# A loop of attention over two-batch groups, reordered into rounds: all half-array matmuls of a round in one run, with four score banks and two query banks

## The reference, cut to what matters

```python
q_big = einsum('bshk,hkq->bshq', (layernorm(x) @ Wq.T).reshape(B, S, H, K), w_kc_q)
q_big = _apply_rope(q_big, sin_q, cos_q)                       # width 192 per head
q_r, k_r = einsum('bshq,hqr->bhsr', q_big, W_qr), einsum('bld,hdr->bhlr', kv_r, W_kr)
attn = softmax(einsum('bhsr,bhlr->bhsl', q_r, k_r))
ctx_c = einsum('bhsl,bld->bhsd', attn, kv_r)
x = x + einsum('bhsd,hkd->bhsk', ctx_c, w_kc_kv)...reshape(B, S, H * K) @ Wo.T
```

## Time and profile before

| | us |
|---|---|
| median of 3 runs | 413.5 |
| lowest, highest | 413.28, 413.62 |
| span of the profiled execution | 411.3 |
| its TensorE busy time | 386.1 (94%) |
| its VectorE busy time | 306.3 (74%) |
| its ScalarE busy time | 216.8 (53%) |
| its GpSimd busy time | 180.6 (44%) |
| the loop's first scores to the last tile of the attention's output | 32.4 to 275.9 |

### The profile page before, as it was taken

One profiled execution on the slowest core, in us unless ns is written; L12 is line 12 of the kernel. 1 busy time (PEld: TensorE's weight loads), 2 busy tenths in 40 slices (PEclk: granted clock), 3 DMA queues, 4 the chain that ended last, 5 costly groups with the idle time before them and its releaser, 6 DMA issues.

```text
span 411.3 us, 6289 instructions
## 1 busy us (share of the span) xinstructions
PE 386.1 (94%) x2121; PEld 257.6 (63%) x2121; DVE 306.3 (74%) x676; ACT 216.8 (53%) x579; POOL 180.6 (44%) x170
## 2 busy tenths in 40 slices
PE   8799899999999999999999999988879988999996
PEld 8675556656666666566655677764245445678886
DVE  5796777877767668776668766646989998898673
ACT  1523655555465657556553876327879532574140
POOL 2554456555646554664656422386530042053200
PEclk9999999999999999999999999999977999999999
DMA  7638001020020030000210000300000000000001
GB/s 254 202 125 328 1 22 81 1 104 2 2 102 2 0 104 1 2 0 0 81 63 0 2 0 0 114 0 2 0 1 0 2 0 0 2 1 2 26 27 52
DMA packets 9087, 17.54 MB, mean 43 GB/s; under 512 B 2144, under 2 KB 6944, under 8 KB 8160
## 3 DMA queue, kind: packets, MB, share of 16 engines
q1 hardware_dynamic: 9056, 17.14, 12.4%
HBM read 16.09 MB, written 1.05 MB: 42 GB/s over the span
## 4 chain that ended last, share of the span: by engine, by line
PE 61%; DVE 22%; ACT 9%; issue 4%; DMA 2%; POOL 1%; SPq 0%; DVEq 0%; ACTq 0%
PE bank L1340 7%; PE bank L1464 7%; PE bank L1458 6%; PE bank L1433 6%; PE bank L1342 6%; PE bank L1341 6%; PE bank L1446 5%; DVE rot_up L891 4%; PE bank L1418 3%; ACT prob L629 3%; PE bank L1363 3%; DVE relu L1050 2%; ACT probT L620 2%; PE bank L1412 2%; DMA blobs<-in_blob 2%
## 5 line engine op out<-in xcount | busy, mean ns | idle before, releaser
L462 POOL TENSOR_TENSOR prob<-prob,rinv 128x512 f32<-128x512 f32 x64 | 67.0, 1048 | 106.5 <-DVE rinv L956 106.5
L629 ACT ACTIVATE prob<-bank,negmax 128x256 f32<-128x256 f32 x128 | 60.1, 480 | 39.8 <-DVE negmax L951 39.8
L951 DVE TENSOR_REDUCE negmax<-bank 128x2 f32<-128x512 f32 x64 | 41.2, 686 | 25.1 <-PE bank L1433 24.6
L620 ACT COPY probT<-bank 128x512 f32<-128x512 f32 x64 | 37.8, 591 | 19.2 <-PE bank L1446 19.0
L457 POOL TENSOR_TENSOR rot_low<-rot_low,rot_up 128x512 f32<-128x512 f32 x32 | 40.8, 1276 | 10.9 <-DVE rot_up L891 10.9
L891 DVE TENSOR_TENSOR rot_up<-bank,cb 64x512 f32<-64x512 f32 x64 | 44.1, 689 | 0.9
L1340 PE MATMUL bank<-xnT,w 128*128 128x512 f32 x96 | 42.0, 437 | 2.2 <-DVE xnT L867 1.7
L1446 PEld LDWEIGHTS bank<-ca,prob 128*128 128x128 f32 x256 | 30.5, 141 | 18.8 <-issue 16.1
L889 DVE TENSOR_TENSOR rot_low<-bank,cb 128x512 f32<-128x512 f32 x32 | 22.0, 688 | 25.2 <-PE bank L1342 25.1
L1446 PE MATMUL bank<-ca,prob 128*128 128x128 f32 x256 | 38.9, 275 | 1.8 <-ACT probT L620 1.1
L442 POOL TENSOR_TENSOR c_y<-c_ve,minus_half 128x4 f32<-128x4 f32 (+1 forms) x9 | 9.8, 1087 | 64.9 <-DVE c_ve L848 52.1
(11 more groups left out here) (213 smaller groups left out, 788.3 us busy)
## 6 DMA issues: line engine op xcount, KB each, us to landing
blobs<-in_blob SPq DMA_DIRECT2D x7, 1024.0 KB, 4.9
xs<-in_x SPq DMA_DIRECT2D x2, 512.0 KB, 4.1
xn<-in_w_fc_t SPq DMA_DIRECT2D x1, 1024.0 KB, 4.8
ctxT<-in_w_proj_t SPq DMA_DIRECT2D x1, 1024.0 KB, 5.5
out<-qk SPq DMA_DIRECT2D x8, 128.0 KB, 1.8
cb<-in_const_b SPq DMA_DIRECT2D x1, 768.0 KB, 8.5
blobs<-in_w_gate SPq DMA_DIRECT2D x1, 704.0 KB, 4.3
blobs<-in_w_up SPq DMA_DIRECT2D x1, 704.0 KB, 5.7
```

The costliest lines, as they stand in the source:

```text
L462: pool.tensor_tensor(p[:], p[:], rinv[:, n % PROBS, :].unsqueeze(2).to_broadcast([P, 2, S]), ALU.mult).then_inc(normed, 1)
L620: act.copy(probT[n % 2][:].rearrange("p a s -> p (a s)"), pT[:]).then_inc(probsT_copied, 1)
L629: ins = act.activation(prob[n % PROBS][:, st, :], pS[n % 2][:, st * S:(st + 1) * S], ACT.Exp, bias=negmax[:, n % 2, st:st + 1], accum_out= ...
L951: dve.tensor_reduce(negmax[:, n % 2, :], pS[n % 2][:].rearrange("p (a s) -> p a s", a=2), AX, ALU.max, negate=True).then_inc(max_ready, 1)
```

## The change

The slots are gone. The loop is written out as rounds, one for each group `g` (0 to 15). On TensorE a round begins with `small_tiles`: `latent_u(g+1, 0)`, fold 3 where there is one, the contexts of both batches of group g-1, the scores of both batches of group g. Then come whole-array matmuls only: `latent_q`, `latent_u(g+1, 1)`, `latent_q`, the first unit's transposes, a fold, the second unit's, `latent_q`, the third's, a fold, the fourth's. The line numbers that follow for the changed kernel are its own: 1536 own product, 1577 contexts, 1552 scores, 1436 to 1438 `latent_q`, 1523 `latent_u(.., 1)`, 1568 transposes, 1470, 1477 and 1481 folds 0 and 1, 2, and 3.

Banks: scores in four (1, 3, 5, 6), one for each unit; `latent_q` alternately in 0 and 7, so that it waits for the rope before the last one; contexts in the transposes' bank 4, both batches in one, copied at once; folds 0 to 2 in `pu` (bank 2), fold 3 in bank 0. Folds 0 and 1 of a pair stand in the even rounds, fold 2 in the odd ones, fold 3 in the even round after. With it come new waits: `prep(p, 1)` and the next round's `latent_u(.., 0)` wait for VectorE's `w1_low` to be through with `pu` (`w1_parts`), and round 13's for the weights' scale (`wscale_ready`). The projection and the weights' casting follow in rounds 14 and 15.

```diff
+UNITS = 4
+PROBS = UNITS
+SCORE_BANK = (1, 3, 5, 6)
...
+def folds_at(g):
+    p = g // 2 + 2
+    if p >= PAIRS:
+        return (None, None)
+    return ((p, 0), (p, 1)) if g % 2 == 0 else ((p, 2), None)
+def late_fold_at(g):
+    p = g // 2 + 1
+    return p if g % 2 == 0 and 2 <= p < PAIRS else None
...
+        pq, pu, pT = [bank[0], bank[7]], bank[2], bank[4]
+        pS, pV, last_pV = [bank[i] for i in SCORE_BANK], bank[4], [bank[5], bank[6]]
         def fold_bank(f, i):
-            return bank[i] if f == 0 and i < 3 else pW
+            if f < 2:
+                return bank[i] if f == 0 and i < 3 else bank[7]
+            return pu if i < 3 else pq[0]
...
+            return bank[Q_BANK[m]] if m < QSTEPS else pq[m % 2]
...
+            for g in range(GROUPS):
+                n = g + 2
+                norm_probs(UNITS * g)
+                norm_probs(UNITS * g + 1)
+                if n < GROUPS:
+                    join(n, 0)
+                norm_probs(UNITS * g + 2)
+                norm_probs(UNITS * g + 3)
+                if n < GROUPS:
+                    join(n, 1)
+                    join(n, 2)
...
+            for g in range(QUIET):
+                n = UNITS * g
+                if late_fold_at(g) is not None:
+                    fold_copy(late_fold_at(g), 3)
+                if g:
+                    context_copy(g - 1)
+                exponentials(n)
+                exponentials(n + 1)
+                exponentials(n + 2)
+                u_copy(g + 1)
+                turned_probs(n)
+                exponentials(n + 3)
+                first, second = folds_at(g)
+                if first is not None:
+                    fold_copy(*first)
+                turned_probs(n + 1)
+                turned_probs(n + 2)
+                if second is not None:
+                    fold_copy(*second)
+                turned_probs(n + 3)
+                if g in WD_ROUNDS:
+                    wd_round(WD_ROUNDS.index(g))
...
+            n = UNITS * QUIET
+            context_copy(QUIET - 1)
+            exponentials(n)
+            exponentials(n + 1)
+            w8_cast(0)
+            exponentials(n + 2)
+            u_copy(QUIET + 1)
+            turned_probs(n)
+            exponentials(n + 3)
+            w8_cast(1)
+            turned_probs(n + 1)
+            w8_cast(2)
+            turned_probs(n + 2)
+            w8_cast(3)
+            turned_probs(n + 3)
+            for j in range(4, W8_PIECES):
+                w8_cast(j)
...
+            for g in range(QUIET):
+                n, m = UNITS * g, RT * (g + 2)
+                first, second = folds_at(g)
+                largest_score(n)
+                largest_score(n + 1)
+                largest_score(n + 2)
+                inverse_sum(n)
+                rope_straight(m)
+                inverse_sum(n + 1)
+                rope_crossed(m)
+                largest_score(n + 3)
+                inverse_sum(n + 2)
+                rope_straight(m + 1)
+                inverse_sum(n + 3)
+                rope_crossed(m + 1)
+                if first is not None and first[1] < 2:
+                    w1_low(*first)
+                if g == SCALE_ROUND:
                     dve.wait_ge(wmax_turned, 1)
-                    in_order(dve.tensor_reduce(wcol[:], pW[:, 0:P], AX, ALU.max))
+                    in_order(dve.tensor_reduce(wcol[:], pu[:, 0:P], AX, ALU.max))
                     dve.tensor_scalar(wdiag[:], ident[:, 0:2], wcol[:], None, ALU.mult).then_inc(wdiag_ready, 1)
-                if s == SCALE_AT + 4:
+                rope(m + 2)
+                if second is not None:
+                    w1_low(*second)
+                if g in (1, 2):
+                    weight_largest(g - 1)
+                if g in WD_ROUNDS:
...
+                elif i == 0:
+                    if f == 1:
+                        pe.wait_ge(wkvo_ready, 1)
+                    else:
+                        pe.wait_ge(u_copied, 2 * f - 2)
+                elif i == 1:
+                    pe.wait_ge(w1_parts, 2 * f + 1)
+                elif i == 2:
+                    if f == 1:
+                        pe.wait_ge(w1_parts, 2 * f + 2)
+                    else:
+                        pe.wait_ge(u_copied, 2 * f - 1)
+                elif f == 1:
                     pe.wait_ge(wqk_ready, f + 1)
-                elif i == 3:
-                    pe.wait_ge(turned_copied, 4)
+                else:
+                    pe.wait_ge(rot_ready, RT * (2 * f - 2) + 5)
...
+                if m > QSTEPS + 1:
+                    pe.wait_ge(rot_ready, m - 1)
+                    if m % RT == 0 and late_fold_at(m // RT - 2) is not None:
+                        pe.wait_ge(wkvo_ready, late_fold_at(m // RT - 2) + 1)
...
+                if 2 <= n < GROUPS - 2:
+                    if n % 2:
+                        pe.wait_ge(wqk_ready, n // 2 + 2)
+                    else:
+                        pe.wait_ge(w1_parts, n + 4)
+                elif n == GROUPS - 2:
+                    pe.wait_ge(wscale_ready, 1)
...
+                    at = a * S + st * P
                     for h in range(2):
                         lo, hi = h * DC, (h + 1) * DC
-                        ins = pe.matmul(pS[h][:, st * S:(st + 1) * S], uT[b // 2][lo:hi, at:at + P],
+                        ins = pe.matmul(pS[2 * a + h][:, st * S:(st + 1) * S], uT[g % 2][lo:hi, at:at + P],
                                         ktmp[lo:hi, b * S:(b + 1) * S], start=True, stop=True)
                         if st == 1:
...
+            def small_tiles(g):
+                if g + 1 < GROUPS:
+                    latent_u(g + 1, 0)
+                if late_fold_at(g) is not None:
+                    prep(late_fold_at(g), 3)
+                if g:
+                    contexts(g - 1)
+                if g == 0:
+                    pe.wait_ge(kv_ready, 2)
+                scores(g, 0)
+                scores(g, 1)
...
+            for g in range(QUIET):
+                n, m = UNITS * g, RT * (g + 2)
+                first, second = folds_at(g)
+                small_tiles(g)
+                latent_q(m)
+                latent_u(g + 1, 1)
+                latent_q(m + 1)
+                turn_probs(n)
+                if first is not None:
+                    prep(*first)
+                if g == SCALE_ROUND:
                     pe.wait_ge(wmax_ready, 2)
-                    pe.wait_ge(wkvo_ready, PAIRS)
-                    pe.transpose(pW[:, 0:P], pad, ident).then_inc(wmax_turned, 1)
-                if s == SCALE_AT + 3:
+                    pe.wait_ge(u_copied, g + 2)
+                    pe.transpose(pu[:, 0:P], pad, ident).then_inc(wmax_turned, 1)
+                turn_probs(n + 1)
+                latent_q(m + 2)
+                turn_probs(n + 2)
+                if second is not None:
+                    prep(*second)
+                if g == SCALE_ROUND:
                     pe.wait_ge(wdiag_ready, 1)
-                    pe.matmul(pW[:, P:P + 2], ones, wdiag[:], start=True, stop=True).then_inc(wmax_here, 1)
-                if s >= LAST_PAIR:
-                    for n in range(AHEAD * (s - LAST_PAIR), AHEAD * (s - LAST_PAIR + 1)):
-                        if n < 6 * (PAIRS - 1):
-                            project_ahead(n)
-                if s > LAST - AHEAD:
-                    for n in range(AHEAD * (s - LAST + AHEAD - 1), AHEAD * (s - LAST + AHEAD)):
-                        if n < 2 * (PAIRS - 1):
-                            project_ahead(6 * (PAIRS - 1) + n)
-                if last_pair_at(s) is not None:
-                    project_last(last_pair_at(s))
-                if batch_at(s) is not None:
-                    if batch_at(s) == 0:
-                        pe.wait_ge(kva_ready, 1)
-                    context(batch_at(s))
-                if unit_at(s - TURN_AFTER) is not None:
-                    turn_probs(unit_at(s - TURN_AFTER))
+                    pe.matmul(pu[:, P:P + 2], ones, wdiag[:], start=True, stop=True).then_inc(wmax_here, 1)
+                turn_probs(n + 3)
...
+            n = UNITS * QUIET
+            small_tiles(QUIET)
+            latent_u(QUIET + 1, 1)
+            ahead(0, 4)
+            turn_probs(n)
+            ahead(4, 8)
+            turn_probs(n + 1)
+            ahead(8, 12)
+            turn_probs(n + 2)
+            ahead(12, 16)
+            turn_probs(n + 3)
+            ahead(16, 34)
...
+            n = UNITS * (QUIET + 1)
+            small_tiles(QUIET + 1)
+            ahead(34, 42)
+            turn_probs(n)
+            ahead(42, 44)
+            turn_probs(n + 1)
+            project_last(0)
+            turn_probs(n + 2)
+            ahead(44, 46)
+            turn_probs(n + 3)
+            project_last(1)
+            last_contexts()
+            ahead(46, 50)
+            project_last(2)
+            ahead(50, NT * (PAIRS - 1))```

```

(56 more changed lines are left out.)

269 lines of the change are left out of this document (107 added, 162 removed).

## The result

The kernel after takes 423.98 us (median of 4 runs, 421.26 to 424.9), the kernel before, measured beside it, 413.39 (4 runs, 413.0 to 413.62): a ratio of 1.0218, with a 95% interval from 1.0164 to 1.0272. It is slower, and the forecast of 424 stands within 0.1. The profiled execution is the quickest of the four: 421.26, with a span of 419.5. Against the span of 411.3 before that is +8.2, where the sum said +11; the agreement of the medians is better than the sum was, and the end of "why" says where the rest lies. Three of the four runs are 2.1 to 3.6 slower than this one, so in what follows gains are read from spans and from the starts of rounds, not from medians alone.

What follows compares the result with a forecast made beforehand. TensorE, nearly always busy, bounds the kernel before; after, chains through the other engines set the rounds. +14.0 to round 14's scores and -3.0 in the tail give +11 on 413.5: 424 forecast, range 412 to 430.

Steps and rivals of the forecast that it cites:

- the sum: Whole profiled execution: +14.0 us up to round 14's scores, -3.0 in the tail, so +11 on the span of 411.3.
- here `w1_low` stands on the path: End of even rounds: both folds' low parts, 0.61 each, hold up the next own product; in bank 7 they cost nobody anything.
- One sign that the prediction named: Wait before the own product: put down to VectorE's line 908 in even rounds, GpSimd's line 448 in odd ones.
- The changes of form: TensorE switching between half-array and whole-array work: eight per group become three, 5.15 becomes 4.74, saving some 0.9 us a group.
- Even rounds: Loop rounds with folds 0 and 1: crossed half ends at 12.90, then low parts, third rope, low parts: 16.3 us.
- Odd rounds: Loop rounds whose next own product waits for GpSimd's join after the crossed half ends at 12.46: 13.9 us.
- TensorE alone: Odd round: TensorE's own work would be through at 12.5, so it stands still for 1.4 us.
- it does what it is built for: Rival: TensorE stays the bound in the loop, pairs of 26.2, whole kernel 394 us; chance 11%.
- Round 12: Next own product waits for the weights' scale: 12.90, small steps some 0.5, rope 2.09, last scale steps 1.1: 16.6 us.
- Round 13: Near the loop's end, taken like round 1: 13.9 us.
- given back: Tail from round 14's scores to the output's last tile: 3.5 less TensorE work, 0.5 of stalls, so 3 us back.
- the clock falls: Rival: stops in the rounds drop TensorE's clock, ten us at half clock per pair, 30 us more, 454; chance 4%.

Runs made afterwards that it cites:

- first experiment: Kernel after the change with folds 1 and 2 exchanged, so fold 1's low parts stand in the odd round: 415.05 us, ratio 1.0052 to the kernel before.
- second experiment: Kernel after the change with the weights' scale split over rounds 12 and 13: 419.62 us, ratio 1.0143 to the kernel before.
- third experiment: Both moves together: kernel after the change with folds 1 and 2 exchanged and the weights' scale split over rounds 12 and 13: 409.94 us, ratio 0.991.
- fifth experiment: Kernel after the change without the low parts of the loop's folds (pairs 2 to 7), output not the reference's: 410.23 us, ratio 0.9932 to the kernel before.
- fourth experiment: Kernel after the change with VectorE's fourth reciprocal behind the crossed half in even rounds: 418.76 us, ratio 1.0137 to the kernel before.
- sixth experiment: Kernel after the change with folds back in bank 7 and one bank for latent_q instead of two: 473.44 us, ratio 1.1431 to the kernel before.

## Why the prediction was right, and where it was not

**The shape.** The order of the waits, the alternation, the run of own product, fold 3 and contexts, and VectorE's 4 us of idleness came as forecast. The first experiment moves the second fold's low parts away, with no work taken out; the waits of 8.4 for them are gone and each even round is 1.3 shorter: the step "here `w1_low` stands on the path" is shown, not only argued. One sign that the prediction named is half right: the wait ahead of the own product is put down to line 908 at the end of even rounds, as forecast, but at the end of odd ones no matmul's wait is put down to line 448; only the load of the own product's weights waits for it, 0.2 in each of seven rounds.

**The changes of form.** Own product, two batches' contexts and scores were to take 4.74; from 134.62 to the next `latent_q` at 139.28 they take 4.66. Against the 5.15 of before the saving is there in full, and by the first transposes the round is 0.2 ahead of the forecast (8.41 and 8.84 after the start, forecast 8.61 and 9.05). Here the trace agrees with the Trainium skill's "TensorEngine Tiling (Array Packing)", Key Properties; and, as the prediction held against it, the rule tells nothing of who waits next.

**Even rounds: 16.06, forecast 16.3.** The 0.2 are those of TensorE's first part; from the transposes on, the chain to the crossed half's end took 3.76 (127.40 to 131.16), forecast 3.85.

**Odd rounds: 13.58, forecast 13.9.** 0.2 again by the early transposes, and 0.1 by a shorter chain. But the term beside it was wrong: TensorE alone was to be through at 12.5, so that it would stand for 1.4. It stands for 0.77 only, and ahead of line 1568. The sum had the last two transposes 0.36 apart. They are 1.37 apart (146.25 to 147.62), since both go through one bank: the second waits until ScalarE has copied the first. That is 1.0; 0.16 more is the fold (0.93, not 0.77) and the rest the starts. With ScalarE's copy in it, TensorE's part alone needs 13.58, not 12.5. The rival "it does what it is built for" was overrated by the same step: its pair of 26.2 takes the odd round at 12.5 and the even one at 13.7. With both moves made the pair is 28.38: 1.1 more in the odd round by the above, and 1.1 more in the even one, 0.6 of it the wait for the first low parts and most of the rest the two folds of 0.93. Whether the join or the copy sets the odd round stays open. They end within 0.05, the matmul rows name the copy and the weight load names the join, and no experiment moved one without the other.

**Round 12: 17.48, forecast 16.6.** The mis-sized term is the small steps of the scale, which were taken from the 0.17 of a reciprocal: 0.5 for two. The profile after (VectorE and GpSimd):

```profile
220.11 0.29 DVE L1055 TENSOR_REDUCE wcol<-bank 128x1 f32<-128x128 f32 x1
220.16 1.26 POOL L448 TENSOR_TENSOR rot_low<-rot_low,rot_up 128x512 f32<-128x512 f32 x1 [0.37 <-DVE rot_up L947]
...
220.44 1.01 DVE L1056 TENSOR_SCALAR wdiag<-ca,wcol 128x2 f32<-128x2 f32 x1
221.36 0.68 DVE L941 TENSOR_TENSOR rot_z<-bank,cb 128x512 f32<-128x512 f32 x1
...
223.52 1.26 POOL L446 TENSOR_TENSOR rot_z<-rot_z 128x512 f32<-128x512 f32 x1 [2.10 <-DVE rot_z L947]
...
223.87 0.94 DVE L1069 TENSOR_SCALAR wsi<-wsi 128x2 f32<-128x2 f32 x1
```

From line 1055's start to the rope's start it is 1.25 instead of 0.5, and line 1069 takes 0.94 where line 983 took 0.72: 1.0 together, with 0.14 of hand-over; the crossed half ends 0.3 earlier than forecast. The operations themselves are not slow. In the kernel before, the one of line 1056 takes 0.23:

```profile
216.94 0.23 DVE L977 TENSOR_SCALAR wdiag<-ca,wcol 128x2 f32<-128x2 f32 x1
```

No operation of GpSimd runs beside it there. After the change one does, and both steps end 0.02 to 0.03 after GpSimd's operation: 221.44 after 221.42, 224.81 after 224.78. The 0.72 before is the same (222.95, GpSimd's ends at 222.93). So 0.5 for the small steps was right for a VectorE that has GpSimd idle beside it. What the sum lacked is that after the change both stand next to a join.

**Round 13: 15.27, forecast 13.9.** In the second and third experiments, where no fall of the clock stands there, the round takes 13.7. The fall costs 1.7, and the last section shows it.

**Sums.** Round 14 starts at 240.22, forecast 241.9; its scores (243.02 in the last chain) come 12.3 later than before, forecast 14.0. The output's last tile (line 1099) is at 284.30, so that scores to last tile take 41.3, before 45.2: 3.9 given back, forecast 3.0. That makes +8.4, the span +8.2.

**The rest of the median.** By the medians the kernel is 10.6 slower, by the spans 8.2. The three runs that were not profiled have spans of 421.6, 422.8 and 423.1 with a mean granted clock of 0.984, 0.975 and 0.976, against 419.5 and 0.988 in the profiled one: the time goes with the clock. The rival "the clock falls" had 4% and a price of 30 us. It was right in kind and far off in size: in the profiled execution one fall in the loop costs 1.7. Where the clock fell in the other three runs no profile tells. The lowest and highest run lie 3.6 apart in the kernel after, 4.0 and 4.2 in the first and fifth experiments, which keep the scale's 2.6 of waiting, and 1.0 and 1.25 in the third and second, which don't. But the kernel before has no such stop either, and its 17 runs beside the experiments lie 3.9 apart; and the part behind the attention, with falls of its own, takes 135.0 to 136.3 in profiled executions of kernels that are alike there. So it stays open whether the clock's loss in those three runs hangs on this stop.

The forecast of the median was thus met by luck, by two errors of opposite sign: the span was forecast 2.8 too long (4.5, had the fall in round 13 not come), and the distance from the profiled span to the median 2.3 too short (2.2 kept, 4.5 measured).

## What to carry to other kernels

When like work is gathered into runs, ask of each bank it shares who reads it last, and where in that engine's queue the reading stands: 0.62 of low parts cost nothing in one round and 1.3 in the other, where a rope of 2.1 came onto the path with them. Two uses of one bank in a row cost the copy between them (1.37 instead of 0.36), even if neither engine is full. When a small step of VectorE is put on the path, look at what GpSimd does at that time: the same step took 0.23 alone and 1.01 beside a join. A saving on the engine that bounds the kernel (here 0.9 a group) is worth only what is left after the chain through the others, so follow that chain to the end of the round before counting it, and move single steps rather than speed them up.

## What the runs showed of the hardware

The granted clock fell behind short stops inside a dense loop. In round 12 of the kernel after TensorE stands for 1.38 (line 1683), works for 0.9, and stands for 2.58 for the scale (stretches: length, PE, PEld, DVE, ACT, POOL; granted clock; and TensorE's rows):

```profile
222.00:224.00 2.00, 0.38 (x4) 0.14 (x2) 1.87 (x6) 0.59 (x1) 0.48 (x1) 1.00 0.04 8
224.00:226.00 2.00, 1.05 (x4) 0.53 (x6) 0.81 (x1) 0.00 (x0) 0.78 (x1) 0.76 0.00 0
226.00:228.00 2.00, 2.00 (x11) 1.06 (x9) 0.00 (x0) 0.00 (x0) 0.00 (x0) 0.50 0.00 0
228.00:230.00 2.00, 2.00 (x18) 1.35 (x16) 0.00 (x0) 0.51 (x1) 0.00 (x0) 0.88 0.00 0
```

```profile
224.95 1.92 PE L1536 MATMUL bank<-rot_low,wqk 128*64 128x512 f32 x4 [2.58 <-DVE wsi L1069]
```

From 226 to 228 the clock is at 0.50, the lower level of 1.2 GHz, although the work is back since 224.95. By starts the own product takes 1.65 and the contexts 2.78, against 0.88 and 1.86 in the odd round above: the 1.7 of round 13. The same loss stands in every profile with the 2.58 stop (first and fifth experiments too, round 13 at 15.2 to 15.3), also after the 1.8 stop of the fourth. After a stop of 1.39 it came once in six in the second experiment's execution (above) and in none of six in the kernel after's; of the sixth experiment's 14 stops of 1.83, each with one of 1.42 some 5 ahead of it, five were followed by a fall. I had expected dense matmuls around a stop to keep the clock. The Trainium skill's "TensorE: Matmul & The Clock Gate", Part 1, has the clock fall after idleness, which agrees in kind. No run here varied a stop's length by itself, so nothing here tells what makes one stop cost the clock and the next, of the same length, not.

The second thing is VectorE beside GpSimd. In all eight profiles the two small multiplications of the scale that read no bank (line 1056's and line 1069's) end 0.02 to 0.03 after the operation of GpSimd that runs when they start, and take 0.72 to 1.03; the one exception, line 977 before, has no such neighbour and takes 0.23. Where the join began earlier against the step (the fourth experiment), the step ended with it all the same and took 0.81. The step that reads a bank (line 1067) and the reciprocal (line 1068) take 0.16 and 0.17 with GpSimd running beside them.
